# First layer: a batch's attention scores issued directly ahead of the products with the values

## The chip, the cores and the metric

The kernel runs on one core of a Trainium2 chip. The metric is the device time of one launch in microseconds (us). Five engines work side by side: TensorE (PE in the profile; PEld is its weight load), VectorE (DVE), ScalarE (ACT), GpSimd (POOL) and SyncE (SP), which here only issues DMAs. Each takes its own instructions in the order written and they meet at semaphores.

## The reference, cut to what matters

Four layers in a row on x (16 batches, 128 tokens, 256 features). The change touches only the first, which computes, per batch:

```
ln  = layernorm(x);  q, k, v = split(ln @ w_qkv + b_qkv)
x   = x + attention(q, k, v, self mask) @ w_ao + b_ao
ln  = layernorm(x);  q = ln @ w_q + b_q;  k, v = split(encoder @ w_kv + b_kv)
x   = x + attention(q, k, v, cross mask) @ w_co + b_co
x   = x + gelu(layernorm(x) @ w1 + b1) @ w2 + b2

attention: scores = q @ k.T / 4 (16 heads of 16 features each)
           probs  = softmax(scores * mask - 10000 * (1 - mask));  out = probs @ v
```

The three later layers (another attention over 16 heads of 64, a single-head attention, a non-local block) are the same before and after.

## The kernel before

**Tiling.** The first layer (function `layer0`) takes the 16 batches as 8 pairs. One attention of a pair has 2 batches x 16 heads; four heads are a unit, so an attention has 8 units, and a step is the passage of one unit through the engines. A unit passes through: its scores on TensorE (`scores`, L624) into one of four PSUM banks; `multiply` by the mask on VectorE (L961), which reads the bank and writes `ring_e`; `add_mask` on GpSimd (L469); `maxima` on VectorE (L971); `exponentials` on ScalarE (L790); `turn` on TensorE (L641), a transpose into the one bank `turn_bank`; `copy_turned` on ScalarE (L797), which empties that bank into `ring_t`. Then, for a batch (four units) at once, `times_v` (L661, the products with the values) and `sums` (L649, the softmax's denominators) on TensorE, `invert` and `divide` on VectorE.

`scores` works for a whole batch: one call writes all four banks with 16 matmuls (32 in the profile, since a float32 matmul shows as two), and waits only that the bank of the unit before it has been read by `multiply`. Its matmuls use 32 of the array's 128 rows each (32*128 in the profile), four side by side. Those of `times_v` and `sums` use 32 columns each (128*32). Transposes and linear maps use the whole array (128*128).

**Software pipeline.** The work of different pairs is interleaved. A body has 16 steps: 8 units of the self attention of one pair and 8 of the cross attention of another. 13 bodies run (g = 0 to 12; 5 to 7 as a loop). `units(stage, s)` issues a stage for unit s of the body (s below 8 cross, from 8 on self, 16 the first of the next body), `pairs(stage, off, ...)` a stage of the pair g + off. A call for a pair that doesn't exist is left out, so bodies 0 to 3 and 8 to 12 are thinner. Every engine has such a `body` of its own (TensorE L677, ScalarE L812, VectorE L1032, GpSimd L486), and each order is written out by hand.

**Linear maps.** The 17 linear results of a body (cv, y0, q, k, T2, f0, y1, f1, o, ck, f2, T1, f3, cq, v, co, T0, in the order of `FILLED`, L231) go alternately to two PSUM banks, 6 and 7. T0, T1 and T2 are transposes of the normalised rows `ln` (`norm_turn`, L540; `normalise` on VectorE, L898). TensorE may fill a bank only when the engine that reads the result before it in that bank is done (`free`, L243). So k waits for the reader of y0 (`output` on VectorE, L952), T2 for the reader of q (ScalarE, L777), co for the reader of cq (ScalarE), T0 for the reader of v (`spread_values` on VectorE, L911). The first scores of an attention also wait for the reads of q and k, or cq and ck (L627).

**Where `scores` stands.** Four calls in TensorE's body: `units(scores, 4)` ahead of k, `units(scores, 8)` ahead of f1, `units(scores, 12)` ahead of turn 8, `units(scores, 16)` ahead of co. 4 and 16 are cross attention, 8 and 12 self attention. On VectorE the first `multiply` of each group stands at a place of its own: `units(multiply, 12)` after `normalise` of T1's rows, `maxima` 10, and so on.

Of the kernel before, what the change touches and what calls it, by code (L numbers as in the profile page):

```python
# [139 lines left out]
def layer0(nc, v):  # L140
# [19 lines left out]
    with ExitStack() as ctx:  # L160
# [166 lines left out]
        def stages(j, g):  # L327


            def units(stage, s):  # L330
                if unit(j, g, s):
                    stage(*unit(j, g, s))

            def pairs(stage, off, *more):
                if pair(j, g, off) is not None:
                    stage(pair(j, g, off), g + off, *more)

            return units, pairs
# [193 lines left out]
        def _(pe):  # L532
# [144 lines left out]
            def body(j, g):  # L677
                units, pairs = stages(j, g)

                units(sums, -8)  # L680
                units(turn, -3)

                pairs(linear, -3, "cv")
                units(turn, -2)
                pairs(linear, -5, "y0")

                pairs(linear, -1, "q")
                units(turn, -1)
                units(scores, 4)

                pairs(linear, -1, "k")
                units(turn, 0)
                pairs(linear, -4, "T2")
                units(times_v, -4)

                units(sums, -4)
                units(turn, 1)

                pairs(linear, -4, "f0")
                units(turn, 2)  # L700
                pairs(linear, -5, "y1")

                units(turn, 3)
                units(scores, 8)

                pairs(linear, -4, "f1")
                units(turn, 4)
                units(times_v, 0)

                units(sums, 0)  # L710
                units(turn, 5)
                pairs(linear, -2, "o")

                units(turn, 6)
                pairs(linear, -2, "ck")

                pairs(linear, -4, "f2")
                units(turn, 7)
                units(scores, 12)

                units(turn, 8)
                pairs(linear, -2, "T1")
                units(times_v, 4)

                units(sums, 4)
                units(turn, 9)
                pairs(linear, -4, "f3")
                pairs(linear, -2, "cq")

                units(turn, 10)  # L730
                pairs(linear, -1, "v")

                units(turn, 11)
                units(scores, 16)

                pairs(linear, -3, "co")
                units(turn, 12)
                pairs(linear, 0, "T0")
                units(times_v, 8)

            pe.wait_ge(consts_made, 1)
            bodies(pe, body)

        @block.scalar
# [1527 lines left out]
```

## Time and profile before

| | |
|---|---|
| median of 3 runs | 1245.84 us (1245.05 to 1247.12) |
| profiled execution | 1245.98 us |
| its span | 1244.2 us |
| mean granted TensorE clock | 0.992 of full speed |
| PE busy | 1176.8 us, 95% |
| PEld busy | 989.1 us, 79% |
| DVE busy | 908.0 us, 73% |
| ACT busy | 818.7 us, 66% |
| POOL busy | 551.7 us, 44% |
| first layer | from 0 to some 462 us, when the next layer's first matmul starts |

Busy times are sums over the whole span, in which the stages have different limits; what the change is worth is read from the first layer. The end of a matmul is modelled by the profiler, so successive starts tell more than durations do. A row of the timeline stands for one or several instructions in a row of one line and kind.

### The profile page before, as it was taken

To read this page: it belongs to the slowest core of one execution; us is meant where nothing else is said; L and a number is where in the kernel's file an instruction comes from. 1 tells how busy PE (TensorE), PEld (TensorE's weight loads), DVE (VectorE), ACT (ScalarE), POOL (GpSimd) and SP (SyncE) were. 2 spreads that over 40 slices of the span, in tenths; PEclk is the share of its full clock that TensorE was granted. 3 is DMA by queue.
4 is the path that set the end of the run, shared out by engine and by line. 5 is a ranking of instruction groups with operands and counts; after the bars stand their busy time and mean duration, and the time that the engine had idled before them with its cause. 6 is when DMAs were issued, how large, how long until landed. Compare 5 with 4: busy or idle time off the path is not lost.

```text
span 1244.2 us, 29755 instructions
## 1 busy us (share of the span) xinstructions
PE 1176.8 (95%) x10914; PEld 989.1 (79%) x10914; DVE 908.0 (73%) x1771; ACT 818.7 (66%) x2459; POOL 551.7 (44%) x535
## 2 busy tenths in 40 slices
PE   4799999999999888899999999999999999999997
PEld 3577788887877677788888888888888888888675
DVE  4779989889897757876667667666767676666564
ACT  3588978989786747566665565566665655656443
POOL 3446556646462326533433433334333334344343
PEclk9999999999999999999999999999999999999999
DMA  3250000000000000000000000000000100000011
GB/s 106 95 222 19 14 14 18 13 13 8 14 11 6 1 19 9 2 10 1 2 10 1 2 10 1 2 10 1 11 1 2 57 1 1 2 1 2 18 50 37
DMA packets 18574, 25.38 MB, mean 20 GB/s; under 512 B 1424, under 2 KB 17040, under 8 KB 17936
## 3 DMA queue, kind: packets, MB, share of 16 engines
q1 hardware_dynamic: 18448, 23.69, 5.8%
q8 instruction: 81, 1.33, 0.4%
q14 instruction: 45, 0.37, 0.1%
HBM read 21.58 MB, written 2.10 MB: 19 GB/s over the span
## 4 chain that ended last, share of the span: by engine, by line
PE 57%; ACT 2%; DVE 2%; issue 1%; DMA 0%; SPq 0%; ACTq 0%
PE psum L1801 14%; PE psum L1853 9%; PE psum L1836 9%; PE psum L1820 8%; PE psum L1803 7%; PE psum L1863 3%; ACT prob L1957 2%; PE psum L1322 1%; PE psum L1386 1%; DVE wzl L2134 1%; PE psum L1336 1%; PE psum L1887 1%; PE psum L1872 1%; PE psum L1879 1%; PE psum L1364 1%
## 5 line engine op out<-in xcount | busy, mean ns | idle before, releaser
L1741 POOL TENSOR_TENSOR prob<-prob,l_z_inv 128x512 f32<-128x512 f32 x256 | 264.8, 1046 | 385.9 <-DVE l_z_inv L2057 385.8
L1957 ACT ACTIVATE prob<-psum,l_neg_max 128x256 f32<-128x256 f32 x512 | 238.9, 481 | 203.4 <-DVE l_neg_max L2050 203.4
L794 ACT ACTIVATE ring_e<-ring_e,neg_max 128x128 f32<-128x128 f32 x512 | 164.3, 406 | 15.1 <-DVE neg_max L973 15.0
L2050 DVE TENSOR_REDUCE l_neg_max<-psum 128x2 f32<-128x512 f32 x256 | 158.7, 683 | 11.2 <-PE psum L1820 11.1
L1836 PE MATMUL psum<-ident,prob 128*128 128x128 f32 x1024 | 134.5, 273 | 7.1 <-ACT prob L1957 7.1
L1836 PEld LDWEIGHTS psum<-ident,prob 128*128 128x128 f32 x1024 | 116.8, 141 | 19.3 <-issue 9.9
L478 POOL TENSOR_TENSOR ring_e<-ring_e,cross_add 128x512 f32<-128x512 f32 x64 | 85.1, 1347 | 91.8 <-DVE ring_e L968 91.8
L1853 PE MATMUL psum<-pT,vs 128*64 128x256 f32 x1024 | 124.6, 385 | 0.0
L478 POOL TENSOR_TENSOR ring_e<-ring_e,self_add 128x512 f32<-128x512 f32 x64 | 85.9, 1356 | 62.1 <-DVE ring_e L968 61.5
L1957 ACT ACTIVATION_READ_ACCUMULATOR prob<-psum,l_neg_max 128x1 f32 x512 | 108.1, 211 | 0.0
L2081 DVE SCALAR_TENSOR_TENSOR kl<-psum,kh 128x512 fp32r<-128x512 f32 x64 | 44.3, 692 | 87.3 <-ACT kh L1979 87.3
L802 ACT COPY ring_t<-psum 128x512 f32<-128x512 f32 x128 | 75.3, 588 | 45.0 <-PE psum L645 44.5
L1853 PEld LDWEIGHTS psum<-pT,vs 128*64 128x64 f32 x1024 | 67.8, 136 | 36.7 <-issue 0.7
L645 PE MATMUL psum<-ident,ring_e 128*128 128x128 f32 x512 | 80.7, 281 | 10.2 <-ACT ring_t L802 9.1
L645 PEld LDWEIGHTS psum<-ident,ring_e 128*128 128x128 f32 x512 | 60.8, 143 | 34.2 <-ACT ring_e L794 12.9
L2062 DVE COPY pT<-psum 128x512 f32<-128x512 f32 x128 | 86.6, 676 | 0.6 <-PE psum L1836 0.6
L973 DVE TENSOR_REDUCE neg_max<-ring_e 128x4 f32<-128x512 f32 x128 | 84.9, 675 | 2.3 <-POOL ring_e L478 2.3
L2077 DVE SCALAR_TENSOR_TENSOR ql<-psum,cols,qh 128x512 fp32r<-128x512 f32 x64 | 48.1, 751 | 46.7 <-ACT qh L1976 45.8
L1820 PE MATMUL psum<-kh,qh 64*128 64x256 f32 x512 | 78.9, 305 | 0.6 <-issue 0.6
L1966 ACT COPY pT<-psum 128x512 f32<-128x512 f32 x128 | 76.0, 594 | 0.3 <-PE psum L1836 0.3
L1976 ACT ACTIVATE qh<-psum,cols 128x512 fp32r<-128x512 f32 x64 | 44.2, 690 | 45.2 <-PE psum L1801 44.3
L1801 PE MATMUL psum<-zuh,wzh 128*128 128x256 f32 x224 | 73.6, 329 | 0.0
(208 smaller groups left out, 3217.1 us busy)
## 6 DMA issues: line engine op xcount, KB each, us to landing
wz_raw<-wz_in SPq DMA_DIRECT2D x2, 1536.0 KB, 14.7
wi_raw<-wi_in SPq DMA_DIRECT2D x2, 1536.0 KB, 20.5
x_in<-x SPq DMA_DIRECT2D x8, 256.0 KB, 2.8
cT<-ctxT SPq DMA_DIRECT2D x8, 256.0 KB, 2.9
w<-w_in SPq DMA_DIRECT2D x2, 1024.0 KB, 8.7
l_ub<-ctx_in SPq DMA_DIRECT2D x8, 256.0 KB, 2.8
cg<-ctx_in SPq DMA_DIRECT2D x4, 512.0 KB, 4.0
out<-fin SPq DMA_DIRECT2D x8, 256.0 KB, 2.1
```

The costliest lines, as they stand in the source:

```text
L478: pool.tensor_tensor(e, e, add, ALU.add).then_inc(scores_add.sem, 1)
L645: last = nc.tensor.transpose(turn_bank[:, h * P:(h + 1) * P], ring_e[:, n % RE, h * P:(h + 1) * P], ident[:, :])
L794: last = nc.scalar.activation(e, e, ACT.Exp, bias=neg_max[:, n % RE, h:h + 1])
L1741: pool.tensor_tensor(e, e, z_inv[:, t % RE, h, :].unsqueeze(2).broadcast_to([P, 2, D]), ALU.mult)\
L1801: last = mm(o, w, zu[xp][:, s, c, :, :].rearrange("p b l -> p (b l)"), **flags)
L1803: last = mm(o, zu[xp][:, s, c, int(name[3]), :], w, **flags)
L1820: last = mm(score_bank[b][h][:, qt * D:(qt + 1) * D], q[qp][rows, qt, b, :], k[kp][rows, :, b, :], start=(qp, kp) == (0, 0), stop=(qp, kp) ...
L1836: last = nc.tensor.transpose(score_bank[b][h][:, kt * D + qt * P:kt * D + (qt + 1) * P], prob[:, t % RE, h, qt * D + kt * P:qt * D + (kt + ...
L1853: last = mm(pv_bank[h * HD1:(h + 1) * HD1, b * D:(b + 1) * D], vs[:, n // 2 % 2, b, kt, at:at + HD1], pT[:, b, h, kt * D:(kt + 1) * D], st ...
L1957: last = nc.scalar.activation(prob[:, t % RE, h, qt * D:(qt + 1) * D], score_bank[b][h][:, qt * D:(qt + 1) * D], ACT.Exp, bias=neg_max[:, ...
L2050: nc.vector.tensor_reduce(neg_max[:, t % RE, h, :], score_bank[b][h].rearrange("p (t c) -> p t c", t=2), AX.X, ALU.max, negate=True).then_ ...
L2062: nc.vector.tensor_copy(pT[:, b, 1, :], score_bank[b][1]).then_inc(copied[1].sem, 1)
```

## The change

In TensorE's body each of the four calls of `scores` is moved down until it stands directly ahead of a call of `times_v`. The orders of the other engines are kept, as is everything that `scores` waits for.

```diff
                 pairs(linear, -1, "q")
                 units(turn, -1)
-                units(scores, 4)
 
                 pairs(linear, -1, "k")
                 units(turn, 0)
                 pairs(linear, -4, "T2")
+                units(scores, 4)
                 units(times_v, -4)
...
                 units(turn, 3)
-                units(scores, 8)
 
                 pairs(linear, -4, "f1")
                 units(turn, 4)
+                units(scores, 8)
                 units(times_v, 0)
...
                 units(turn, 7)
-                units(scores, 12)
 
                 units(turn, 8)
                 pairs(linear, -2, "T1")
+                units(scores, 12)
                 units(times_v, 4)
...
                 units(turn, 11)
-                units(scores, 16)
 
                 pairs(linear, -3, "co")
                 units(turn, 12)
                 pairs(linear, 0, "T0")
+                units(scores, 16)
                 units(times_v, 8)
```

## Rows read from the trace of the kernel before

**Rows 1.** The profile page, first part: busy us, share of the span, instructions.

```profile
PE 1176.8 (95%) x10914; PEld 989.1 (79%) x10914; DVE 908.0 (73%) x1771; ACT 818.7 (66%) x2459; POOL 551.7 (44%) x535
```

**Rows 2.** Engines by stretch, full body: window, length, busy us, PEclk, DMA, GB/s.

```profile
280.32:331.14 50.82, 49.73 (x525) 41.21 (x524) 45.05 (x83) 43.36 (x118) 29.01 (x25) 1.00 0.04 14
```

**Rows 3.** TensorE's timeline around scores 8: start, length, line, tiles, count, idle before.

```profile
279.79 0.60 PE L645 MATMUL psum<-ident,ring_e 128*128 128x128 f32 x4
280.32 1.17 PE L635 MATMUL psum<-kT,qT 32*128 32x128 f32 x32
281.42 1.99 PE L556 MATMUL psum<-lnT,w 128*128 128x256 f32 x8
283.25 0.60 PE L645 MATMUL psum<-ident,ring_e 128*128 128x128 f32 x4
283.78 1.08 PE L672 MATMUL psum<-ring_t,cvm 128*32 128x128 f32 x32
```

**Rows 4.** VectorE's timeline in the half body after scores 8.

```profile
281.66 0.68 DVE L968 TENSOR_TENSOR ring_e<-psum,self_mul 128x512 f32<-128x512 f32 x1
...
285.80 1.76 DVE L979 RECIPROCAL z_inv<-psum 128x256 f32<-128x256 f32 x1 [0.47 <-PE psum L655]
...
291.76 2.64 DVE L902 TENSOR_SCALAR ln<-x,mean_var,rstd 128x256 f32<-128x256 f32 x2
```

**Rows 5.** TensorE's timeline around scores 12: f2, turn 7, scores, turn 8, T1, times_v.

```profile
290.30 1.89 PE L556 MATMUL psum<-lnT,w 128*128 128x256 f32 x8
292.02 0.60 PE L645 MATMUL psum<-ident,ring_e 128*128 128x128 f32 x4
292.55 1.17 PE L635 MATMUL psum<-kT,qT 32*128 32x128 f32 x32
293.66 0.66 PE L645 MATMUL psum<-ident,ring_e 128*128 128x128 f32 x4
294.53 0.65 PE L547 MATMUL psum<-ident,ln 128*128 128x128 f32 x4 [0.22 <-DVE ln L902]
295.12 1.08 PE L672 MATMUL psum<-ring_t,cvm 128*32 128x128 f32 x32
```

**Rows 6.** ScalarE's timeline: copy of turn 7, read of cq, copy of turn 11.

```profile
292.66 0.59 ACT L802 COPY ring_t<-psum 128x512 f32<-128x512 f32 x1 [0.17 <-PE psum L645]
...
302.49 1.96 ACT L750 ACTIVATE cqT<-psum,bq_scaled,parity 128x256 f32<-128x256 f32 x4
...
306.51 0.60 ACT L802 COPY ring_t<-psum 128x512 f32<-128x512 f32 x1
```

**Rows 7.** TensorE's timeline around scores 16: scores, turn 12, times_v.

```profile
304.58 1.17 PE L635 MATMUL psum<-ckT,cqT 32*128 32x128 f32 x32 [0.87 <-ACT cqT L750]
...
307.51 0.60 PE L645 MATMUL psum<-ident,ring_e 128*128 128x128 f32 x4
...
308.48 1.08 PE L672 MATMUL psum<-ring_t,vm 128*32 128x128 f32 x32
```

**Rows 8.** Timeline of all engines around scores 4, and VectorE's next idle time.

```profile
318.08 0.41 DVE L957 SCALAR_TENSOR_TENSOR xs<-psum,x_mlp 128x256 f32<-128x256 f32 x1
318.19 0.60 PE L645 MATMUL psum<-ident,ring_e 128*128 128x128 f32 x4
318.73 1.17 PE L635 MATMUL psum<-ckT,cqT 32*128 32x128 f32 x32
...
319.31 1.94 ACT L750 ACTIVATE qT<-psum,bq_scaled,parity 128x256 f32<-128x256 f32 x4
...
319.92 1.89 DVE L968 TENSOR_TENSOR ring_e<-psum,cross_mul 128x512 f32<-128x512 f32 x3 [0.83 <-PE psum L635]
...
329.45 0.43 DVE L936 TENSOR_SCALAR ring_g<-ring_g 128x512 f32<-128x512 f32 x1 [1.59 <-ACT ring_g L761]
```

**Rows 9.** Engines in two stretches (columns as in Rows 2).

```profile
80.00:84.00 4.00, 2.32 (x36) 1.29 (x24) 2.96 (x5) 4.00 (x13) 2.03 (x3) 1.00 0.00 1
84.00:88.00 4.00, 3.90 (x48) 3.15 (x52) 2.18 (x4) 2.92 (x10) 1.18 (x2) 0.57 0.13 37
```

## The prediction

> **What bounds the kernel now.** I read the page's busy shares first: PE 95%, DVE 73% [rows 1]. Those are averages, so the stretches came next. A full body of the first layer takes 50.82 us, with PE busy 49.73, DVE 45.05, ACT 43.36 and POOL 29.01 us, at full clock [rows 2]; the two bodies ahead of it take 50.88 and 50.90 (same view). TensorE is the bound with about 1 us idle, and VectorE is 5.8 us behind it: close enough that a late VectorE can hold TensorE up. So what counts is not how much work is issued (nothing is added or removed) but whether an engine finds its input ready. For that I read the timelines of all engines through this body. Below, "scores 8" means the call `units(scores, 8)`; times are those of the span.
>
> **Tile modes.** Successive starts show what a change of the array's shape costs. f1, right behind scores, takes 1.83 us to the next start, f2, behind a linear map, 1.72 [rows 3, 5]: 0.11. From a transpose to the next start it is 0.53 where scores follow [rows 3]. What is new is a start of times_v behind scores, 32*128 to 128*32, which the trace doesn't have. Bounds: nothing, or the 0.11 of 32*128 to 128*128. I take 0.11, the row in which scores are left: then scores still take 1.10 us to the next start [rows 3], and each group saves the way from a transpose into times_v and keeps the rest, 0.1 us; with the other bound 0.2. There are 8 pairs x 2 attentions x 2 batches = 32 groups: 3 to 6 us gained over the layer.
> The Trainium skill, "TensorEngine Tiling (Array Packing)", section "Key Properties", says that a change of tiling mode drains TensorE. By it four changes per group become three, which is all in favour of the change; it gives the rival "faster" below, and the trace agrees that there is a cost, at 0.11 us.
>
> **What the move takes away.** Scores come 2 to 3 us later for VectorE, and the work that filled TensorE's waits stands elsewhere. Four places, in order.
>
> *Scores 8.* New order: turn 3 at 279.79, f1, turn 4, scores, times_v. f1 starts 0.44 behind the turn (the step without a change of shape, 0.53 less 0.09) and takes 1.72, so turn 4 at 281.95, scores at 282.48, times_v at 283.58 against 283.78: 0.2 us gained. VectorE's first multiply needs the first bank, 1.19 us behind the start of scores (scores at 318.73, multiply at 319.92 after waiting [rows 8]): 283.67 against 281.66, 2.0 us late. Its order is kept, so gated 0, the other multiplies and two maxima queue behind it. The reciprocal had 0.47 us idle before it [rows 4], which absorbs that much. What is left is 1.54 us, and between the reciprocal and normalise 1 the timeline shows no idle time on VectorE, so normalise ends at 294.40 + 1.54 = 295.94. POOL's mask additions follow the multiplies and have room (29 of 50.8 us busy); POOL's reciprocal root for normalise 1 follows the same VectorE work. SP's next mask load waits for a multiply too, but is a whole body ahead. No DMA moves.
>
> *Scores 12.* This is the costly one. T1 today waits for ln, 0.22 us, although scores 12 stand ahead of it and fill 1.1 us [rows 5]. In the new order turn 8 follows turn 7 at once and must wait until ScalarE has emptied turn_bank: turn 7 at 291.82, its copy ends about 1.2 us after its start as today (292.02 to 293.25 [rows 5, 6]), turn 8 at 293.05. Then T1 waits for ln until 296.07, then scores 0.53 later, times_v 1.10 after that: 297.70 against 295.12. So from 0.2 early TensorE is 2.6 us late, 1.1 for scores that no longer hide anything, the rest VectorE's lag. VectorE's multiply 12 comes at 296.6 + 1.19 = 297.8 against 294.92 on the timeline: lag 2.9.
>
> *Scores 16.* They wait 0.87 us for ScalarE's read of cq [rows 7]. That looks like a wait that later scores would avoid. But co, now first, fills the bank that cq was in and waits for the same read. It starts at 304.6 in today's times, turn 12 could follow at 306.3, and there ScalarE's copy of turn 11, which ends at 307.11 [rows 6], holds it; so 307.15, T0, scores 308.1, times_v 309.25 against 308.48 [rows 7]: 0.75 us more, lag 3.35. Multiply 16 then comes 4.6 us late on VectorE (311.9 for 307.33 on the timeline).
>
> *Scores 4.* k needs y0's bank, which VectorE's output frees at 318.49 [rows 8], 4.6 later 323.1. TensorE would be there at 318.63 + 3.35 = 322.0: 1.1 us of new wait. T2's wait for the read of q, which ends at 321.25 [rows 8], is then covered. times_v at 326.9 for 322.63 on the timeline: lag 4.3. VectorE, now some 5.5 late at the reciprocal of this batch, catches up at the polynomial of f0, which has 1.59 us idle before it [rows 8] and is itself 4.3 later: the next body starts evenly. So a full body costs 4.3 us: -0.2, +2.8, +0.75, +0.95.
>
> **Sum.** The pair (scores 12, scores 16) meets this pattern in bodies 3 to 8: 6 x (2.6 + 0.75) = 20.1 (each body starts anew at a gain of 0.2, included). Scores 4 in five of them: 5 x 0.95 = 4.8. Bodies 1, 2, 9 and 10 have few stages beside the scores: scores 8 of bodies 1 and 2 don't move against anything, scores 12 of body 2 leave a stall for ln and scores 16 slip behind T0; body 10 waits for ln at T2; I put 1 us on all. Together 26.
>
> **The clock.** Falls of the clock follow idle stretches: PE busy 2.32 of 4 us, then 0.57 of full speed over the next 4 us, part of them at the lower level of 1.2 GHz: a loss of 1.7 us [rows 9]. The new wait at T1 is 2.5 us behind one of 0.8, in six bodies. Bounds: no fall, 0; a fall each, 6 x 1.7 = 10. Part of each would lie in the stall itself, so I take 5 us, the middle. 26 + 5 = 31 over the profiled execution's 1245.98 us (span 1244.2 and 1.8 around it; the median 1245.84 is the same within 0.2): 1277. The thinner bodies 3 and 8 have less VectorE work in the chain, worth some 2 us: 1275.
>
> **Rivals.**
> *Only the primary loss.* VectorE's lag of 1.5 us is caught up before normalise 1, and T1 finds ln at 294.53 as today. For: each POOL-bound VectorE instruction could run shorter (normalise takes 2.64 us for two instructions [rows 4]; 0.73 where POOL is idle, at 305.43 on the timeline). Against: no idle time stands in that chain. Then a body costs 1.1 + 0.75 - 0.2 = 1.65, six of them 10: 1256.
> *Cascade.* The clock falls in most bodies and its 1.7 us delays ScalarE's and VectorE's chains again, a second fall at scores 16 included: 26 + 6 x 3.4 = 46: 1292. For: VectorE 45.05 of 50.82 busy [rows 2]. Against: much of it lies in stalls.
> *Faster.* Fewer drains decide, 32 x 0.1 to 0.2 us, and the read of cq is out of the way, 6 x 0.9 = 5: at best 1235 to 1243, say 1241. It decides only from the point where ln is ready before turn 8 ends, near 293.5; today it is ready at 294.40 [rows 4, 5], so VectorE would have to be 0.9 us earlier, while its multiplies come later. And co must not need the bank of cq, which it does.
> *Nothing.* The shift is absorbed: 1246, if gains in shape just pay the wait at T1 (6 x 1.1 against 3 to 6 us).
>
> **How the numbers follow.** Forecast (1266 to 1284) 0.50; only the primary loss 0.24 (1250 to 1262); cascade 0.16; nothing 0.04; faster 0.06. A change under 0.2%, 2.5 us, can't be told from none. Slower then has 0.90, within 0.2% 0.04, faster 0.06. The time is 1275; the range, reaching into both neighbours and leaving out about 2 in 10, 1252 to 1293.
>
> **What would show it.** In the timeline of the kernel after: T1 (L547 behind L645) with idle time of 2 us or more put down to ln L902, and turn 8 with some 0.7 put down to ring_t L802; DVE L968 waiting for L635 before each of the four first multiplies; k (L556) waiting for xs L957; a full body of 55 to 57 us; granted clock below 1.00 in stretches of bodies 3 to 8. Scores followed by times_v 1.0 to 1.1 us later. It is wrong if T1's wait stays near 0.2 us, if co starts without waiting for cqT, or if the layer's end (the next layer's first matmul) moves by less than 5 us; a later layer that changes its length would be outside of it altogether.

## The result and the profile after

The changed kernel takes 1293.87 us (median of 4 runs, 1292.6 to 1295.83) beside 1245.44 us for the kernel before: ratio 1.0382, 95% interval 1.0368 to 1.0395, 48.4 us slower. The forecast was 1275 with a range to 1293. The direction was right, and each wait that was named is there; the size was too small by 19 us. The time is near that of the rival "cascade" (1292), but not for its reason: that rival had two falls of the clock in a body, the second at scores 16, and the full bodies have one each, behind T1. Its number is met by luck.

The page's first part of the kernel after [rows 1]. The span goes from 1244.2 to 1294.1 us. The busy sums of the other engines move by at most 4.3 us; PE's grows by 18.3 us with the same number of instructions, since more of them run at half clock (mean granted clock 0.978 for 0.992).

```profile
PE 1195.1 (92%) x10914; PEld 1001.1 (77%) x10914; DVE 912.3 (71%) x1771; ACT 818.9 (63%) x2459; POOL 549.5 (42%) x535
```

The first layer in three stretches, cut where scores 8 of body 3 and of body 8 start, before and then after (columns as in [rows 2]):

```profile
0.00:84.70 84.70, 56.60 (x577) 44.33 (x577) 53.80 (x100) 50.71 (x136) 37.52 (x49) 0.94 0.43 154
84.70:331.14 246.44, 238.36 (x2565) 196.51 (x2564) 217.21 (x397) 211.00 (x576) 141.22 (x125) 0.99 0.05 15
331.14:462.53 131.39, 118.05 (x1053) 95.35 (x1053) 103.55 (x177) 93.48 (x247) 50.54 (x46) 0.99 0.02 4
...
0.00:90.72 90.72, 60.23 (x580) 47.46 (x580) 54.17 (x100) 52.44 (x141) 37.59 (x49) 0.89 0.40 145
90.72:369.90 279.18, 250.22 (x2574) 203.86 (x2573) 222.15 (x398) 211.52 (x577) 138.62 (x124) 0.96 0.04 13
369.90:511.22 141.32, 119.55 (x1041) 95.33 (x1041) 102.67 (x174) 91.20 (x243) 50.49 (x46) 0.96 0.01 4
```

Two thirds of the loss, 32.7 us, lie in bodies 3 to 7, 6.0 us ahead of them and 9.9 us from body 8 on (the move itself puts both cuts some 2 us later in their body). The granted clock is lower in all three stretches. Counted in steps of 1 us, the layer has 17 us at half clock before and 51 us after, in stretches of 3.4 us or twice or three times that; bodies 3 to 8 have a new one each behind T1.

One full body (body 7) by stretch [rows 2], and below it the 3.4 us behind T1:

```profile
312.14:369.90 57.76, 51.89 (x526) 42.38 (x525) 45.85 (x82) 43.62 (x120) 28.38 (x25) 0.97 0.04 12
...
326.33:329.74 3.41, 3.41 (x68) 3.05 (x68) 1.81 (x4) 2.29 (x7) 1.17 (x2) 0.50 0.00 0
```

57.76 us for 50.82: 6.94 more. PE's busy time grew by 2.2 us with the same work, since 3.4 us of the body now run at half clock, 1.2 GHz; the other 4.8 us are idle. VectorE's busy time grew by 0.8.

TensorE's timeline of that body, the places of [rows 3, 5, 7, 8] in turn:

```profile
309.88 1.89 PE L556 MATMUL psum<-lnT,w 128*128 128x256 f32 x8
311.61 0.60 PE L645 MATMUL psum<-ident,ring_e 128*128 128x128 f32 x4
312.14 1.17 PE L635 MATMUL psum<-kT,qT 32*128 32x128 f32 x32
313.25 1.08 PE L672 MATMUL psum<-ring_t,cvm 128*32 128x128 f32 x32
...
321.70 0.60 PE L645 MATMUL psum<-ident,ring_e 128*128 128x128 f32 x4
323.06 0.63 PE L645 MATMUL psum<-ident,ring_e 128*128 128x128 f32 x4 [0.77 <-ACT ring_t L802]
325.47 0.65 PE L547 MATMUL psum<-ident,ln 128*128 128x128 f32 x4 [1.77 <-DVE ln L902]
326.05 1.89 PE L635 MATMUL psum<-kT,qT 32*128 32x128 f32 x32
327.87 1.94 PE L672 MATMUL psum<-ring_t,cvm 128*32 128x128 f32 x32
...
338.14 1.99 PE L565 MATMUL psum<-wco,coT 128*128 128x256 f32 x8 [0.80 <-ACT cqT L750]
340.89 0.63 PE L645 MATMUL psum<-ident,ring_e 128*128 128x128 f32 x4 [0.76 <-ACT ring_t L802]
341.89 1.17 PE L635 MATMUL psum<-ckT,cqT 32*128 32x128 f32 x32
342.99 1.08 PE L672 MATMUL psum<-ring_t,vm 128*32 128x128 f32 x32
...
348.68 3.69 PE L565 MATMUL psum<-w,hid 128*128 128x256 f32 x16 [0.99 <-DVE x L928]
...
355.31 1.99 PE L556 MATMUL psum<-lnT,wqkv 128*128 128x256 f32 x8 [0.78 <-DVE xs L957]
```

Read the brackets: turn 8 waits for the copy of turn 7, T1 for ln, co for the read of cq, turn 12 for the copy of turn 11, k for y0's reader, as forecast. Not forecast: y0 waits 0.99 us for `x` (add_product on VectorE, which reads co's bank). And scores 12 take 1.82 us to the next start instead of 1.10, at half clock. Two of the prediction's signs are missed by a little: T1's wait is 1.77 us where 2 or more was named, because ln is ready 0.26 us earlier and turn 8 starts 0.35 us later than worked out, and the body is 57.8 us where 55 to 57 was named.

VectorE (and one row of GpSimd) in the same body [rows 4, 8]:

```profile
313.33 0.69 DVE L968 TENSOR_TENSOR ring_e<-psum,self_mul 128x512 f32<-128x512 f32 x1 [1.93 <-PE psum L635]
316.92 1.75 DVE L979 RECIPROCAL z_inv<-psum 128x256 f32<-128x256 f32 x1
322.70 2.63 DVE L902 TENSOR_SCALAR ln<-x,mean_var,rstd 128x256 f32<-128x256 f32 x2
327.93 1.88 DVE L968 TENSOR_TENSOR ring_e<-psum,self_mul 128x512 f32<-128x512 f32 x3 [2.00 <-PE psum L635]
343.17 0.69 DVE L968 TENSOR_TENSOR ring_e<-psum,cross_mul 128x512 f32<-128x512 f32 x1 [2.73 <-PE psum L635]
343.77 2.37 DVE L948 SCALAR_TENSOR_TENSOR hid<-ring_g,ring_h 128x512 f32<-128x512 f32 x2
343.94 1.65 POOL L478 TENSOR_TENSOR ring_e<-ring_e,cross_add 128x512 f32<-128x512 f32 x1 [7.68 <-DVE ring_e L968]
...
354.84 0.41 DVE L957 SCALAR_TENSOR_TENSOR xs<-psum,x_mlp 128x256 f32<-128x256 f32 x1
359.30 1.29 DVE L968 TENSOR_TENSOR ring_e<-psum,cross_mul 128x512 f32<-128x512 f32 x2 [3.45 <-PE psum L635]
366.04 0.43 DVE L936 TENSOR_SCALAR ring_g<-ring_g 128x512 f32<-128x512 f32 x1 [0.54 <-ACT ring_g L761]
```

Turn 3 ahead of this body starts at 309.45 where it was 279.79, so subtracting 29.66 gives each row's own delay. VectorE: multiply 8 +2.01 (forecast 2.01), reciprocal +1.46 (1.54), normalise +1.28 (1.54), multiply 12 +3.35 (2.9), multiply 16 +6.18 (4.6). TensorE's times_v: -0.19 (-0.2), +3.09 (+2.6), +4.85 (+3.35), +6.9 (+4.3; it starts at 359.21).

The next layer starts at 511.2 us instead of 462.5: 48.7 of the 49.9 us that the span grew lie in the first layer.

### The profile page after: what moved, and what is told of

Same layout as the page of the kernel before. It is cut to its first block, busy times and chain, and to the rows that moved or that the text cites. A ratio compares the mean times of both kernels' runs of the same rounds, so it can differ in the third digit from the quotient of the medians.

```text
span 1294.1 us, 29755 instructions
## 1 busy us (share of the span) xinstructions
PE 1195.1 (92%) x10914; PEld 1001.1 (77%) x10914; DVE 912.3 (71%) x1771; ACT 818.9 (63%) x2459; POOL 549.5 (42%) x535
## 4 chain that ended last, share of the span: by engine, by line
PE 55%; ACT 2%; DVE 2%; issue 1%; DMA 0%; SPq 0%; ACTq 0%
PE psum L1801 14%; PE psum L1853 9%; PE psum L1836 8%; PE psum L1820 7%; PE psum L1803 7%; PE psum L1863 3%; ACT prob L1957 1%; PE psum L1322 1%; PE psum L1386 1%; DVE wzl L2134 1%; PE psum L1336 1%; PE psum L1887 1%; PE psum L1872 1%; PE psum L1879 1%; PE psum L1364 1%
```

## The experiments

Besides the medians (with the ratio to the kernel before and its interval) the table gives the length of one full body, from scores 8 to scores 8, and where a half-clock stretch lies in it. It is body 7 everywhere, taken from the same rows of each trace as the body above. The kernel before was measured again beside each of them, with medians from 1246.4 to 1248.6 us, so the ratios compare better than the medians.

| kernel | median us | ratio | body 7, us | half clock in body 7 |
|---|---|---|---|---|
| before | 1245.44 | | 50.82 | none |
| after | 1293.87 | 1.0382 (1.0368 to 1.0395) | 57.76 | 3.4 us behind T1 |
| scores 8 alone | 1256.80 | 1.0084 (1.0068 to 1.0101) | 52.11 | none |
| scores 12 alone | 1255.79 | 1.0085 (1.0068 to 1.0102) | 51.91 | none |
| scores 16 alone | 1259.28 | 1.0114 (1.0088 to 1.0140) | 52.93 | none |
| scores 4 alone | 1248.39 | 1.0021 (1.0011 to 1.0030) | 51.27 | none |
| scores 16, gated ahead | 1252.58 | 1.0051 (1.0034 to 1.0067) | 51.70 | none |
| after, idle time filled | 1285.63 | 1.0306 (1.0286 to 1.0326) | 56.18 | none |
| after, VectorE's order fitted | 1275.47 | 1.0220 (1.0198 to 1.0242) | 55.21 | 3.4 us |
| after but for scores 8 | 1277.82 | 1.0245 (1.0225 to 1.0264) | 54.88 | none |
| after but for scores 12 | 1278.56 | 1.0248 (1.0232 to 1.0264) | 55.06 | none |
| values up, 4, 8, 12 | 1259.78 | 1.0092 (1.0078 to 1.0107) | 51.71 | none |
| values up, 8, 12 | 1249.66 | 1.0015 (1.0005 to 1.0024) | 50.60 | none |
| values up, 8 | 1248.28 | 1.0007 (0.9998 to 1.0015) | 50.64 | none |
| change in bodies 0 to 2 | 1251.37 | 1.0036 (1.0023 to 1.0050) | as before | none |
| change in bodies 9 to 12 | 1251.93 | 1.0042 (1.0027 to 1.0057) | as before | none |

**The four moves one by one.** Each kernel has one of the four `+units(scores, n)` of the change and its `-` line, the rest as before; for scores 8:

```diff
                 units(turn, 3)
-                units(scores, 8)
 
                 pairs(linear, -4, "f1")
                 units(turn, 4)
+                units(scores, 8)
                 units(times_v, 0)
```

> Only scores 8 are moved. Theory A (VectorE's lag is handed on): TensorE itself gains 0.2 us per body, but the multiplies of the group start 2.0 us late, 1.3 us of it reach ln, and T1 waits some 1.5 us instead of 0.2: about 1.1 us in each of six bodies, 7 us, and up to 6 us more where the clock falls for it: 1252 to 1259, with DVE L902 as the releaser of T1. Theory B (each place costs only the stall seen at that place): no stall is seen at this place in the changed kernel, so 1243 to 1246.

> Only scores 12 are moved. Theory A: VectorE isn't late before T1, so T1 waits for ln as before (starts where it did), turn 8 waits 0.75 us for ScalarE, and scores 12 cost their own 1.1 us: 6 bodies x 1.1 = 7, plus the clock where the two waits together (1.8 us) make it fall (0 to 9 us): 1251 to 1261. Theory B: as in the changed kernel, 3.3 to 4 us at this place per body, 20 us or more: 1265 to 1270.

> Only scores 16 are moved. Theory A: co waits for the read of cq where scores did, turn 12 waits for the copy of turn 11: 0.75 us per body, VectorE 2 us late but with room: 6 x 0.75 = 4.5: 1248 to 1252. Theory B: 0.9 us here and the waits of y0 and k that the changed kernel shows behind it, 2.1 us more per body: 18 us, 1262 to 1265.

> Only scores 4 are moved. Theory A: T2 waits up to 0.5 us for the read of q, less 0.1 to 0.2 of tile changes; VectorE's lag of 3 us is absorbed by its 1.65 and 1.59 us of idle time: five bodies x 0.3 = 1.5: 1244 to 1249. Theory B the same. If the four single moves sum to 48 us, the parts are independent; theory A says they sum to 20 to 35.

Measured: +10.5, +10.6, +14.2 and +2.6 us by the ratios, 38 together beside 48. Scores 8 settle the lag theory: at its own place no stall is seen, and yet the kernel loses 0.8% (theory B said no change). Its body 7 shows the way from the late multiply (2.01 us later than before, counted from turn 3) to ln (1.28 us later) to T1:

```profile
290.68 0.69 DVE L968 TENSOR_TENSOR ring_e<-psum,self_mul 128x512 f32<-128x512 f32 x1 [1.94 <-PE psum L635]
300.05 2.64 DVE L902 TENSOR_SCALAR ln<-x,mean_var,rstd 128x256 f32<-128x256 f32 x2
302.83 0.65 PE L547 MATMUL psum<-ident,ln 128*128 128x128 f32 x4 [1.49 <-DVE ln L902]
```

Scores 12 lose 1.09 us a body, theory A's number, and not B's 3 to 4. In scores 16 both theories missed: 2.11 us a body, where A had 0.75. And the sum of the four is above theory A's 20 to 35 and below 48. So two things stay: what is in scores 16, and 2.0 us a body (6.94 less 1.29 + 1.09 + 2.11 + 0.45) that appear only in the whole.

**Scores 16 and the gated calls.** Scores 16 are moved as in the kernel with that move alone, and on VectorE two `gated` calls go from behind multiply 16 to ahead of it (a body's -4 there is the next body's -5):

```diff
-                pairs(gated, -5, 2)
-                pairs(gated, -5, 3)
                 units(multiply, 1)
...
                 units(maxima, 14)
+                pairs(gated, -4, 2)
+                pairs(gated, -4, 3)
                 units(multiply, 16)
```

> Only scores 16 are moved, and on VectorE the two gated calls (2 and 3) that stood behind multiply 16 stand ahead of it, in the 2.1 us in which it waits for the scores. Theory A (the unforeseen part of scores 16 is a collision: gated, with two SBUF inputs, now starts together with GpSimd's first mask addition, takes 1.1 us longer, and with multiply 16's 2 us makes y0 wait for x): y0's wait of 0.8 to 1.0 us per body goes, the two gated take 1.3 us together instead of 2.4: 1259 becomes 1250 to 1254. Theory B (y0 waits because co itself comes late on TensorE): no change, 1257 to 1260.

Measured 1252.58, body 51.70 instead of 52.93: theory A. In scores 16 alone y0 waits 0.99 us for x as in the changed kernel, and here it doesn't wait. VectorE's and GpSimd's timeline of this kernel at that place:

```profile
310.91 1.28 DVE L948 SCALAR_TENSOR_TENSOR hid<-ring_g,ring_h 128x512 f32<-128x512 f32 x2
...
313.10 1.89 DVE L968 TENSOR_TENSOR ring_e<-psum,cross_mul 128x512 f32<-128x512 f32 x3 [0.91 <-PE psum L635]
...
313.87 2.51 POOL L478 TENSOR_TENSOR ring_e<-ring_e,cross_add 128x512 f32<-128x512 f32 x2 [7.07 <-DVE ring_e L968]
```

Two gated take 1.28 us and two mask additions 2.51. Where gated follow the multiply, they meet GpSimd's addition, which the multiply released. The kernel before has this meeting too, but there GpSimd usually pays (3.51 us for two additions), and only in its body 8 VectorE (2.37 us for two gated):

```profile
307.93 1.28 DVE L948 SCALAR_TENSOR_TENSOR hid<-ring_g,ring_h 128x512 f32<-128x512 f32 x2
308.09 3.51 POOL L478 TENSOR_TENSOR ring_e<-ring_e,cross_add 128x512 f32<-128x512 f32 x2 [4.86 <-DVE ring_e L968]
...
357.82 2.37 DVE L948 SCALAR_TENSOR_TENSOR hid<-ring_g,ring_h 128x512 f32<-128x512 f32 x2
```

In the moved kernels VectorE pays in each full body looked at. The Trainium skill, "SBUF — State Buffer", section "Who interferes with whom", says that a VectorE instruction with two SBUF inputs contends with a GpSimd instruction that reads SBUF. The traces agree, at 1.1 us (2.37 for 1.28). Which of the two is stretched differs between two traces with the same distance between the starts (0.16 us in the kernel before, 0.17 in the changed one); what decides it stays open. Nor do these runs separate the 1.1 us from the 1.3 us that gated no longer stand behind a late multiply: both fell with the one edit.

**The clock.** An extra pass of scores 12 whose end is signalled to nobody, twice, in the idle time:

```diff
                 units(turn, 7)
+                units(fill, 12)
 
                 units(turn, 8)
+                units(fill, 12)
                 pairs(linear, -2, "T1")
                 units(scores, 12)
```

> The changed kernel with two extra passes of scores 12 whose result nobody is told of (it is overwritten by the real ones): one between turn 7 and turn 8, one between turn 8 and T1, in the 2.5 us that TensorE idles there. Theory A (the falls of the clock at scores 12 come from that idle time and cost 1.4 us a body): the half-clock stretch behind T1 is gone in the full bodies, which shrink from 57.8 to some 56.5 us; 1294 becomes 1283 to 1289. Theory B (the lower clock falls where TensorE's work is slack anyway, so it costs nothing): time as the changed kernel or 0 to 4 us more: 1292 to 1298.

Measured 1285.63: 8.2 us faster than the changed kernel (9.5 by the ratios) although the profile counts 512 matmuls more (11426 for 10914), and no half clock in the full bodies: theory A. Bodies 4 to 7 shrink by 1.39 to 1.58 us each. Body 7 of this kernel:

```profile
308.06:364.24 56.18, 52.46 (x590) 43.02 (x589) 45.89 (x82) 43.58 (x120) 28.39 (x25) 1.00 0.04 12
```

**VectorE's order fitted.** TensorE's order is the changed one.

```diff
                 units(maxima, 6)
+                pairs(gated, -4, 0)
+                units(maxima, 7)
                 units(multiply, 8)
...
                 units(maxima, 10)
+                units(maxima, 11)
+                pairs(first_statistics, 0)
                 units(multiply, 12)
...
                 units(maxima, 14)
+                pairs(gated, -4, 2)
+                pairs(gated, -4, 3)
                 units(multiply, 16)
```

(each also taken out of its old place)

> The changed kernel with VectorE's order fitted to it: gated 0 and maxima 7 ahead of multiply 8, maxima 11 and the next pair's statistics ahead of multiply 12, gated 2 and 3 ahead of multiply 16. TensorE's order is that of the changed kernel. Theory A (most of the loss is VectorE's lag, handed on, and the clock that falls for it): a body loses only what TensorE's own order costs, -0.2 +1.1 +0.75 +0.4 = 2 us: 1256 to 1264. Theory B (the loss is TensorE's own order, T1 and turn 8 and co waiting in place of the scores): 1280 or more.

Measured 1275.47: 18 us won back by VectorE's order alone (20 by the ratios), but 11 us above theory A's range. Theory A's 2 us a body became 2.7 where the clock held, and this trace has the price of a fall in two neighbouring bodies, 55.21 and 53.61 us (before: 50.82 and 50.88):

```profile
250.12:303.73 53.61, 49.96 (x526) 41.03 (x525) 45.62 (x83) 43.33 (x119) 27.67 (x25) 1.00 0.04 12
303.73:358.94 55.21, 51.36 (x525) 42.43 (x524) 45.83 (x84) 43.51 (x120) 27.68 (x25) 0.97 0.04 13
```

Same kernel, same work, 0.97 or 1.00 of the clock: 1.6 us. T1 still waits 1.10 us there behind turn 8's 0.77, and a fall follows in bodies 4, 5, 7 and 8, and not in 6. The rest of the miss is in the first bodies: scores 8 of body 3 start at 91.44 instead of 84.70.

**Does the fall need both moves?** The changed kernel with one of its calls put back:

```diff
                 units(turn, 3)
+                units(scores, 8)
 
                 pairs(linear, -4, "f1")
                 units(turn, 4)
-                units(scores, 8)
                 units(times_v, 0)
```

and, in the other kernel,

```diff
                 units(turn, 7)
+                units(scores, 12)
 
                 units(turn, 8)
                 pairs(linear, -2, "T1")
-                units(scores, 12)
                 units(times_v, 4)
```

> The changed kernel with scores 8 back in their old place (12, 16 and 4 moved). Additive theory: 1294 less the 10.5 us of scores 8 alone: 1283. Theory A (the surplus of the whole over its four parts, some 12 us, is the clock that falls only when the lag from scores 8 and the waits at scores 12 meet): no fall of the clock at scores 12 in the full bodies, and 1270 to 1277.

> The changed kernel with scores 12 back in their old place (8, 16 and 4 moved). Additive theory: 1294 less the 10 us of scores 12 alone: 1284. Theory A (the clock falls only where the lag of scores 8 meets the waits of scores 12): no fall in the full bodies behind T1, a body loses some 4 us: 1271 to 1278.

Measured 1277.82 and 1278.56, both just above theory A's ranges and 5 us below the additive ones (6 to 7 by the ratios). The second has no fall in bodies 4 to 7. The first has none in 5 to 7, where turn 8 waits 0.77 us and T1 0.52, but one in body 4 (56.78 us), where T1 waits 0.76. So scores 8 need not be moved for a fall; with scores 12 alone the same two waits in body 4 (0.77 and 0.75) bring none. Body 7 of the first:

```profile
300.11:354.99 54.88, 50.27 (x526) 41.16 (x525) 46.12 (x83) 43.48 (x118) 28.43 (x25) 1.00 0.04 13
```

Three moves lose 4.06 and 4.24 us in body 7, within 0.4 of the sums of their single losses (3.65 and 3.85). The fourth adds its 1.1 to 1.3 and the fall's 1.6. So the body's 6.94 are 4.94 for the four moves, 1.6 for the clock, and 0.4 not assigned.

**The ends.** `if g <= 2:` around the new places and `if not (g <= 2):` around the old ones; the same with g >= 9.

> The change in bodies 0 to 2 alone, the kernel before from body 3 on. In the changed kernel scores 8 of body 3 stand 6.0 us later than before, where the prediction had 1 us for both ends of the layer. Theory A (the thin bodies have TensorE waiting on VectorE and ScalarE in any case, and scores 12 and 16, 6 us later there, stretch that chain and the half clock with it): 1251 to 1255, scores 8 of body 3 at 89 to 92 us instead of 84.7. Theory B (those 6 us are a phase that a following body of the old order wins back from its idle time): 1246 to 1249.

> The change in bodies 9 to 12 alone. Theory A (co, now ahead of scores 16, holds them back from VectorE, whose add_product and the first y0 wait behind: 4.4 us between body 9's second times_v and the end of the layer in the changed kernel): 1249 to 1252. Theory B (the tail waits for something else): 1245 to 1248.

Measured +4.5 and +5.2 us by the ratios (intervals 2.9 to 6.2 and 3.4 to 7.1): theory A for both. In the first kernel's trace scores 8 of body 3 stand at 91.73, 7.0 us later than before, and those of bodies 4 to 8 5.9 us later: body 3 wins 1.1 us back, and the others nothing. The mean granted clock up to body 3 is 0.89 there for 0.94 before, so part of this loss can be the clock; no run separates it. At the other end, in the changed kernel, co waits 2.18 us and then runs at half clock, and y0 waits 3.06 us for x:

```profile
442.07 3.46 PE L565 MATMUL psum<-wco,coT 128*128 128x256 f32 x8 [2.18 <-ACT cqT L750]
...
451.76 5.38 PE L565 MATMUL psum<-w,hid 128*128 128x256 f32 x16 [3.06 <-DVE x L928]
```

In the kernel before it is scores 16 that wait there, 2.08 us, with a half clock behind them as well, and y0 follows at once. So y0's wait is what is new. The kernel with the change in bodies 9 to 12 alone shows both waits (2.17 and 3.05 us) and no half clock from body 8 to the end of the layer; its profiled execution, 2.6 us below its median, has 2.9 us of loss in that stretch.

**The other way round: values up to the scores.**

```diff
                 units(turn, 7)
                 units(scores, 12)
+                units(times_v, 4)
+                units(sums, 4)
 
                 units(turn, 8)
                 pairs(linear, -2, "T1")
-                units(times_v, 4)
-                units(sums, 4)
-                units(turn, 9)
                 pairs(linear, -4, "f3")
+                units(turn, 9)
```

(groups 8 and 4 alike, with turn 4 ahead of f1 and turn 0 ahead of k)

> The other way to bring the two together: scores stay where the kernel before has them (so VectorE's multiplies are not late) and the products with the values and the sums of groups 4, 8 and 12 move up, right behind scores; turn 0 goes ahead of k, turn 4 ahead of f1, turn 9 behind f3, so that no two transposes wait for one copy. Scores 16 is left alone. Theory A (the tile change saved is real, about 0.2 us a group, and only the late signal to VectorE cost time): three groups x 0.2 and T1's wait of 0.4 us, together 1.0 us a body: 1239 to 1243. Theory B (any pairing of the two makes a queue wait: times_v must wait for the copy of the turn just ahead of scores): 1247 to 1252.

> As the kernel with the values moved up, but for groups 8 and 12 alone: group 4 is left as in the kernel before, since there times_v and sums hid the 1.0 us from T2 to f0. Theory A (tile changes saved are real, 0.2 us a group): 0.2 to 0.4 us a body where nothing new waits: 1243 to 1247 beside 1246 to 1248 for the kernel before. Theory B (the read of cq sets the pace behind group 12, so that what is gained ahead of it is lost at scores 16): no change at scores 16 and 4, 0.2 us a body at most from group 8: within 1 us of the kernel before.

> Group 8 alone moved up. Theory A and B: 0.2 us a body, 1.6 us in all, 0 to 2 us faster than the kernel before; slower only if the first bodies, where the clock falls, shift.

Measured 1259.78, 1249.66 and 1248.28. The first missed both theories: in group 4 the two calls had hidden the way from T2 through ScalarE to f0, and f0 now waits, a cost I hadn't seen and theory B didn't name:

```profile
280.40 0.60 PE L547 MATMUL psum<-ident,ln 128*128 128x128 f32 x4
...
282.48 1.99 PE L556 MATMUL psum<-lnT,w 128*128 128x256 f32 x8 [1.05 <-ACT lnT L747]
```

Without group 4 a full body is 0.2 us shorter than before (50.60 and 50.64 for 50.82), which is the saving of tile changes, and the second pair moved adds nothing to it, as theory B had it: scores 16 wait 1.11 us for the read of cq where they waited 0.87. Bodies 3 and 4 lose 0.8 to 1.2 us each. As times, both miss what was expected: the second kernel is 1.9 us slower by the ratio, where theory B had 1 us at most and theory A a gain, and the third, at 1.0007, can't be told from the kernel before. No version tried beats the kernel before.

## Why the prediction was right in kind and wrong in size

The waits that it named are there, in their order. What failed is the sum, in four of its terms: the ends of the layer (1 us, measured some 10), scores 16 (0.75 us a body, measured 2.11), the clock (5 us, measured 8 to 10) and the 2 us taken off.

- *TensorE the bound, VectorE close behind, a late VectorE handed on.* Right, and shown by scores 8 alone: 2.0 us of lag, 1.3 of it at ln, 1.29 us lost a body. VectorE didn't catch up ahead of ln, which rules out the rival "only the primary loss" (1256).
- *Tile modes.* Right at the bound taken: times_v start 1.11 us behind scores (312.14 to 313.25), so 32*128 to 128*32 costs as much as to 128*128, and 0.2 us is saved (-0.19 at scores 8; 0.18 to 0.22 a body in the last two kernels). The prediction contradicts itself here: its paragraph on tile modes has 0.1 us for this bound, and its working at scores 8 has 0.2. The rival "faster" had the right sign for this part alone.
- *Scores 12.* Right: forecast 1.1 for scores that hide nothing, measured 1.09 alone; in the whole T1 stands +1.28 us where +1.54 was forecast.
- *Scores 16.* Wrong by a factor of three: "0.75 us more" was 2.11 alone. Turn 12's and co's waits were as worked out, and 0.88 us a body are left where gated stand ahead of the multiply; left out were gated's collision with GpSimd and y0's wait for the bank of co. I had taken multiply 16's lag to its end at k, and not to the reader of co that stands between.
- *Scores 4.* 0.95 us a body in the sum, 0.45 alone, where the lag of the other moves is missing; its share in the whole wasn't measured by itself. k's wait for y0's reader was forecast and is there (0.78 us, forecast 1.1).
- *The clock.* The mechanism was right, its price was mis-sized. "The middle", 5 us, was taken because part of each fall would lie in the stall itself. Bodies 3 to 8 have a new one each, and where it can be priced it costs 1.4 to 1.6 us, so 8 to 10 us: close to the upper bound. The half clock lies behind T1, on scores 12 and times_v, and not in the stall. The two waits behind turn 7 were forecast at 3.3 us together and are 2.5.
- *The ends.* "I put 1 us on all": some 10, 4.5 in bodies 0 to 2 and 5.2 from body 9 on, each by its own run. This term had no row behind it, and it is half of the miss: 9 of 19 us. The reasoning was that thin bodies have few stages beside the scores. But TensorE waits there in a chain through VectorE and ScalarE, of which scores are the first link; y0's 3.06 us are such a wait. That this chain, and not the clock, makes up most of the 4.5 us in bodies 0 to 2 is argued and not shown.
- *2 us taken off for bodies 3 and 8*: no ground in the traces.

The sum with measured terms: single moves 6 x 4.9 = 30 for bodies 3 to 8 (the losses of body 7, taken for all six), clock 6 x 1.6 = 10, ends 10, together 50, against 48.4 measured.

## What to carry to other kernels

An instruction that only feeds another engine is not free to slide within its own engine's order: its place is the release time of everything queued behind the waiting instruction, so follow the lag to every bank and buffer that the late engine has to free, not just to the next stage. Two waits close together on TensorE can cost more than their sum, by a fall of the clock: 0.77 and some 1.7 us brought one in every full body, while a single wait of 1.49 us (scores 8 alone) brought none. Where a new wait comes to stand behind another, price the fall as the likely case. Work out the ends of a pipeline from their rows like the middle: engines that idle there idle in a chain.

## What the runs showed of the hardware that was not expected

- 512 instructions of work more made a kernel 8.2 us faster (1285.63 for 1293.87), by keeping TensorE at 2.4 GHz: 1.00 instead of 0.97 of the clock over a body.
- Where VectorE's two gated and GpSimd's mask addition overlap, one or the other is stretched. In the kernel before, body 7 has the two gated unstretched at 1.28 us and two additions at 3.51 instead of 2.51; body 8 has the two gated at 2.37.
